# One ViT block with a mixture of experts on one core: the dense part rebuilt as one pipeline over token groups

## The chip, the cores and the metric

The kernel runs on one core of a Trainium2 chip. The metric is device time in microseconds (us), the median over runs of one execution each. TensorE is called PE below, VectorE DVE, ScalarE ACT, GpSimd POOL, and SP is the engine that issues most DMAs.

## What is computed

```python
h = patchify(x) @ W_proj.T + b_proj + pos_emb          # 16 images, 36 patches of 768 numbers, D = 256
h = concatenate([cls_tok, h])                          # 37 tokens an image, 592 in all
q, k, v = split(layernorm(h) @ Wq.T), ... Wk, ... Wv   # 4 heads of 64
attn = softmax(causal(q @ k.T)) @ v                    # within an image
sq = elu(q) + 1
A_mem = (sq @ mem) / (sq @ z + 1e-6)
out = (sigmoid(betas) * A_mem + (1 - sigmoid(betas)) * attn) @ Wo.T + bo
h = h + out
xn = layernorm(h) * gamma + beta                       # in the block: of h, then again in the experts' part
logits = xn @ router_w.T; two experts a token of 8, at most 185 tokens an expert, in token order
h = h + sum over the token's experts of weight * ((silu(xn @ Wg) * (xn @ Wu)) @ W3)
```

## The kernel before, in words

The tokens lie in 6 groups of three images: 111 rows in groups 0 to 4 and 37 in group 5. There are three stages, and each engine has its own program; they meet at semaphores alone. Everything on one engine runs in the order in which it is written.

**Embedding and value projection (lines 323 to 373 on PE).** `embed(g)` multiplies a group's patches with the patch weights: 6 slices of the 768 inputs, each as three passes (lines 335 to 337), because both sides are split into a rounded part and a rest (`x_hi` by ACT, line 611, `x_lo` by DVE, line 779). DVE adds the positions (line 800), takes mean and variance (802 to 804), POOL takes the root (986), DVE normalises into `hn` (773), PE turns it (348), ACT copies it (598) and DVE keeps the rest of it (785). `value(g)` is three passes over two slices (362 to 364). The weights of q, k and v are split too, by ACT (621) and POOL (983). The loop has group t in `embed`, t-1 in `turn_hn` and t-2 in `value`. DVE splits x two groups ahead of its sum: `x_lo` of groups 0 and 1 stands before the first `h` (793, 794).

**Query, key and memory, over all tokens (375 to 423).** Four blocks of 296 columns each for q and for k (386 to 388), the feature map on DVE and ACT, then the memory's denominator for each head as 24 small matmuls (399), its reciprocal on DVE as 111 rows of 24 numbers (850), a transpose (409), a spread over the head's 64 rows (421), and the memory's own matmul (422).

**Attention and routing (425 to 508).** A pipeline over the groups: `score` (mask and four heads), DVE's `row_max` (838), ACT's `softmax` (651), DVE's `normalise` (863 to 865), `turn_probs` (447), `attend` (457), DVE's `add_memory` (875), `project` (467), DVE's `residual` with the second statistics (882 to 888), POOL's root (1007), DVE's `norm2` (893), `turn_xn` (477), ACT's `copy_xnT` (671), `route` (484), DVE's `rank` (899 to 908), `count` (492 to 496), DVE's `send` (913 to 916), and POOL's two indirect DMAs a group (999), which put the token rows into per-expert areas in HBM. The order of each engine's stages in a step is a list of (lag, stage) pairs, written by hand:

```python
for t in range(GROUPS + 7):
    for lag, stage in ((6, route), (3, turn_probs), (4, project), (6, count), (5, turn_xn), (0, score), (3, attend)):
```

After the last group PE runs `keep_busy` (562), the rows come back (306) and the experts' stage (513 to 584) runs to the end. It starts with the transposes of line 520.

## Time and profile before

| | us |
|---|---|
| median of 3 runs | 250.87 |
| lowest, highest | 250.58, 252.39 |
| the profiled execution | 252.72 |
| its span, first to last instruction | 250.8 |
| PE busy, share of the span | 213.8, 85% |
| DVE, ACT, POOL busy | 88.2, 77.0, 55.0 |

The profile is of one execution. Its span is what the rows below are times in; 1.9 us lie outside it. Line numbers are those of the kernel before. A row of a timeline has start, duration, engine, line, operation, what it writes and reads, and in brackets the idle time before it and what ended it. Busy times of PE contain modelled ends, so a busy PE is not a PE at its peak.

### The profile page before, as it was taken

To read this page: it belongs to the slowest core of one execution; us is meant where nothing else is said; L and a number is where in the kernel's file an instruction comes from. 1 tells how busy PE (TensorE), PEld (TensorE's weight loads), DVE (VectorE), ACT (ScalarE), POOL (GpSimd) and SP (SyncE) were. 2 spreads that over 40 slices of the span, in tenths; PEclk is the share of its full clock that TensorE was granted. 3 is DMA by queue.
4 is the path that set the end of the run, shared out by engine and by line. 5 is a ranking of instruction groups with operands and counts; after the bars stand their busy time and mean duration, and the time that the engine had idled before them with its cause. 6 is when DMAs were issued, how large, how long until landed. Compare 5 with 4: busy or idle time off the path is not lost.

```text
span 250.8 us, 3563 instructions
## 1 busy us (share of the span) xinstructions
PE 213.8 (85%) x1307; PEld 189.1 (75%) x1307; DVE 88.2 (35%) x277; ACT 77.0 (31%) x226; POOL 55.0 (22%) x55
## 2 busy tenths in 40 slices
PE   0185957989998984879999999999999999999970
PEld 0175947954766553449999999999999999999960
DVE  6849874442688644302211111111211112111110
ACT  2433312632574112212722222332222323222230
POOL 0245343000004444400003104013040040220404
PEclk9999997975599555599999999999999999999997
DMA  7936995410001221157619239076191580410101
GB/s 244 332 117 130 326 347 231 210 81 1 0 21 46 90 60 49 54 148 200 259 18 400 88 136 379 4 303 231 27 432 52 199 322 0 167 11 0 22 9 16
DMA packets 10299, 36.15 MB, mean 144 GB/s; under 512 B 3328, under 2 KB 6738, under 8 KB 7978
## 3 DMA queue, kind: packets, MB, share of 16 engines
q1 hardware_dynamic: 7514, 31.90, 35.4%
q0 software_dynamic: 2336, 2.13, 4.3%
q10 hardware_dynamic: 432, 1.90, 2.0%
q8 instruction: 10, 0.16, 0.2%
q14 instruction: 7, 0.06, 0.1%
HBM read 31.42 MB, written 5.35 MB: 147 GB/s over the span
## 4 chain that ended last, share of the span: by engine, by line
PE 72%; DVE 9%; DMA 7%; issue 4%; POOL 3%; ACT 2%; POOLq 1%; SPq 1%
PE bank L536 33%; PE bank L548 16%; DMA x_flat<-in 5%; PE bank L467 3%; PE bank L520 3%; DVE hn L773 2%; PE bank L422 2%; PE bank L559 1%; POOL rstd L986 1%; POOL token_rows L999 1%; PE bank L447 1%; PE bank L386 1%; PE bank L387 1%; PE bank L388 1%; PE bank L421 1%
## 5 line engine op out<-in xcount | busy, mean ns | idle before, releaser
L536 PE MATMUL bank<-xb,w 128*128 128x185 f32 x512 | 91.4, 321 | 1.1 <-ACT xb L695 1.1
L536 PEld LDWEIGHTS bank<-xb,w 128*128 128x128 f32 x512 | 81.9, 190 | 1.6 <-issue 1.2
L957 DVE TENSOR_TENSOR hid<-bank,sg 128x185 f32<-128x185 f32 x64 | 22.5, 351 | 113.9 <-ACT sg L707 113.9
L548 PE MATMUL bank<-hid,w 128*128 128x185 f32 x256 | 50.2, 319 | 0.0
L1016 POOL DMA_INDIRECT out<-yw,slot_token x16 | 23.8, 1490 | 119.2 <-ACT yw L727 116.8
L707 ACT ACTIVATE sg<-bank 128x185 f32<-128x185 f32 x64 | 20.9, 327 | 89.1 <-PE bank L536 89.1
L548 PEld LDWEIGHTS bank<-hid,w 128*128 128x128 f32 x256 | 42.1, 189 | 0.0
L335 PE MATMUL bank<-wp_hi,x_hi 128*111 128x256 f32 x36 | 11.2, 310 | 12.6 <-DVE x_lo L779 12.6
L335 PEld LDWEIGHTS bank<-wp_hi,x_hi 128*111 128x111 f32 x36 | 7.0, 194 | 12.9 <-issue 12.9
L999 POOL DMA_INDIRECT token_rows<-rowbuf,dest x12 | 11.6, 969 | 15.1 <-DVE dest L916 13.3
L1007 POOL TENSOR_TENSOR rstd<-var,minus_half 111x1 f32<-111x1 f32 (+1 forms) x6 | 3.5, 576 | 35.0 <-DVE var L888 34.9
L336 PE MATMUL bank<-wp_lo,x_hi 128*111 128x256 f32 x36 | 10.9, 303 | 0.0
L337 PE MATMUL bank<-wp_hi,x_lo 128*111 128x256 f32 x36 | 10.9, 303 | 0.0
L467 PE MATMUL bank<-w_sb,x_flat 128*111 128x256 f32 (+1 forms) x24 | 9.9, 557 | 0.1
L695 ACT ACTIVATE xb<-bank,beta_t,gamma_t 128x185 f32<-128x185 f32 x16 | 7.2, 505 | 8.9 <-PE bank L520 8.9
L671 ACT ACTIVATE xnT<-bank,beta_t,gamma_t 128x111 f32<-128x111 f32 (+1 forms) x12 | 4.6, 433 | 15.2 <-PE bank L477 15.2
L348 PE MATMUL bank<-ident,hn 111*128 111x111 f32 (+1 forms) x12 | 2.2, 267 | 7.2 <-DVE hn L773 7.2
L986 POOL TENSOR_TENSOR rstd<-var,minus_half 111x1 f32<-111x1 f32 (+1 forms) x6 | 5.5, 913 | 11.8 <-DVE var L804 11.8
L773 DVE TENSOR_SCALAR hn<-h,mv,rstd 111x256 f32<-111x256 f32 (+1 forms) x6 | 7.5, 1243 | 1.6 <-POOL rstd L986 1.4
L651 ACT ACTIVATE x_flat<-bank,negmax 111x111 f32<-111x111 f32 (+1 forms) x24 | 7.8, 340 | 0.1
L520 PE MATMUL bank<-ident,rows_in 128*128 128x128 f32 (+1 forms) x32 | 7.5, 285 | 0.2 <-DMA rows_in<-token_rows 0.2
L520 PEld LDWEIGHTS bank<-ident,rows_in 128*128 128x128 f32 (+1 forms) x32 | 4.4, 137 | 4.1 <-issue 1.5
(139 smaller groups left out, 266.7 us busy)
## 6 DMA issues: line engine op xcount, KB each, us to landing
w<-in SPq DMA_DIRECT2D x8, 2048.0 KB, 10.2
w<-in SPq DMA_DIRECT2D x8, 1024.0 KB, 4.8
x_flat<-in SPq DMA_DIRECT2D x6, 333.0 KB, 11.0
token_rows<-rows_in SPq DMA_DIRECT2D x1, 1728.0 KB
rows_in<-token_rows SPq DMA_DIRECT2D x8, 144.0 KB
w_sb<-in ACTq DMA_DIRECT2D x1, 1024.0 KB, 8.8
wp_sb<-in ACTq DMA_DIRECT2D x1, 768.0 KB, 5.6
out<-h SPq DMA_DIRECT2D x5, 111.0 KB
```

Of the source, the lines that this page charges most:

```text
L335: pe.matmul(o, x_hi[g % 2][:, k, :], wp_hi[:, k, :], start=(k == 0), stop=False)
L336: pe.matmul(o, x_hi[g % 2][:, k, :], wp_lo[:, k, :], start=False, stop=False)
L337: mm = pe.matmul(o, x_lo[g % 2][:, k, :], wp_hi[:, k, :], start=False, stop=(k == KE - 1))
L467: mm = pe.matmul(bank[WO_BANK][0:R, 0:D], aoT[:, g % 2, k, 0:R], w_sb[:, 3, k, :], start=(k == 0), stop=(k == 1))
L520: tr = pe.transpose(bank[XB_BANK][:, k * D + s * P:k * D + s * P + n], rows_in[0:n, e, s, k * P:(k + 1) * P], ident[0:n, 0:n])
L536: mm = pe.matmul(o, w[:, part, k, :], xb[b][:, k, :], start=(k == 0), stop=(k == KD - 1))
L548: mm = pe.matmul(bank[YT_BANK[k]][:, 0:NS], w3[e % 2][:, fc, k * P:(k + 1) * P], hid[:, step % 4, :], start=(fc == 0), stop=(fc == FC - 1))
L707: act.activation(sg[:, step % 2, :], bank[GU_BANK[step % len(GU_BANK)]][:, 0:NS], ACT.Silu).then_inc(silu_done, 1)
L773: dve.tensor_scalar(hn[0:R, g, :], h[0:R, g, :], mv1[0:R, g, 0:1], rstd1[0:R, g:g + 1], ALU.subtract, ALU.mult).then_inc(hn_done, 1)
L957: dve.tensor_tensor(hid[:, step % 4, :], bank[GU_BANK[step % len(GU_BANK)]][:, NS:2 * NS], sg[:, step % 2, :], ALU.mult).then_inc(hid_done, 1)
L999: pool.indirect_dma_start(out=rows_dram, out_offset=bass.IndirectOffsetOnAxis(ap=dest[0:n, g, k:k + 1], axis=0), in_=rowbuf[0:n, g, :], in ...
L1016: pool.indirect_dma_start(out=out, out_offset=bass.IndirectOffsetOnAxis(ap=slot_token[0:n, e, s:s + 1], axis=0), in_=yw[b][s][0:n, :], in_ ...
```

## The change

The three-stage dense part becomes one loop of 9 steps. In step t a group t is embedded, group t-1 gets its query, key, value, scores and memory, group t-2 its softmax, attention and output projection, and group t-3 its routing. Every engine has one list of stages. The bank map gives most stages one bank where they had two.

- q, k, v and the memory are computed per group with plain fp32 matmuls (`w_sb`, `hnT`), so the splits of `hnT` (785) and of the q, k, v weights (621, 983) go.
- The memory's denominator is computed with a block-diagonal `z_bd`, which gives it spread over 128 rows and two head pairs. ACT copies it (`copy_den`), DVE takes the reciprocal of 128 rows of 222 numbers in `memory_part`. The gate is multiplied into `mem_bd` once (`setup`).
- The output bias, added to `h` by POOL before (991), is two one-row matmuls in `project`.
- x is split one group ahead, not two: on DVE `split_next` stands behind `first_sum`, `stats1` and `setup`.
- Six loads leave SP's queue, five are issued by ACT ahead of its first work.
- POOL's `root2(t-3)` stands behind the `send` of the step before.
- On PE `project` and `count` stand ahead of `score`; on DVE `row_max` stands last.

```diff
-        S_BANK = ((0, 1), (2, 3))
-        PT_BANK = 4
-        PV_BANK, WO_BANK = 5, 6
-        ROUTER_BANK = 7
+        PV_BANK, K_BANK, T_BANK, ROUTER_BANK, S_BANK, E_BANK, WO_BANK = 0, 1, 2, 3, (4, 5), 6, 7
+        V_BANK, Q_BANK, MEM_BANK, PT_BANK = T_BANK, E_BANK, K_BANK, WO_BANK
...
-            sp.dma_start(mask[:, :], c_mask).then_inc(in_attn, 16)
-            sp.dma_start(bo_b[:, :], bo.partition_broadcast(G_ROWS)).then_inc(in_attn, 16)
-            sp.dma_start(gate[:, :], betas.partition_broadcast(G_ROWS)).then_inc(in_attn, 16)
-            sp.dma_start(z_sb[:, :, :], z4).then_inc(in_attn, 16)
-            sp.dma_start(mem_bd[:, :, :], mem_diag).then_inc(in_attn, 16)
-            sp.dma_start(head_rows[:, :, :], c_head).then_inc(in_attn, 16)
...
             def embed(g):
+                if g >= 1:
+                    pe.wait_ge(h_copied, g)
                 if g >= 2:
-                    pe.wait_ge(h_copied, g - 1)
-                o = bank[E_BANK[g % 2]][0:G_ROWS, 0:D]
+                    pe.wait_ge(q_done, g - 1)
+                o = bank[E_BANK][0:G_ROWS, 0:D]
...
-                if g >= 2:
-                    pe.wait_ge(hnT_lo_done, g - 1)
+                if g >= 1:
+                    pe.wait_ge(v_done, g)
...
             def value(g):
-                full = slice(g * G_ROWS, (g + 1) * G_ROWS)
+                R = ROWS[g]
                 pe.wait_ge(hnT_done, g + 1)
-                pe.wait_ge(hnT_lo_done, g + 1)
                 if g == 0:
-                    pe.wait_ge(w_hi_done, 1)
-                    pe.wait_ge(w_lo_done, 1)
-                if g >= 2:
-                    pe.wait_ge(v_done, g - 1)
-                o = bank[V_BANK[g % 2]][0:G_ROWS, 0:D]
+                    pe.wait_ge(in_w, 16)
                 for k in range(KD):
-                    pe.matmul(o, hnT_hi[:, k, full], w_hi[:, 2, k, :], start=(k == 0), stop=False)
-                    pe.matmul(o, hnT_hi[:, k, full], w_lo[:, 2, k, :], start=False, stop=False)
-                    mm = pe.matmul(o, hnT_lo[:, k, full], w_hi[:, 2, k, :], start=False, stop=(k == KD - 1))
+                    mm = pe.matmul(bank[V_BANK][0:R, 0:D], hnT[:, k, cols(g)], w_sb[:, 2, k, :], start=(k == 0), stop=(k == KD - 1))
                 mm.then_inc(v_in_psum, 1)
...
+            def project_in(o, which, g):
+                R = ROWS[g]
+                for m in range(2):
                     for k in range(KD):
-                        pe.matmul(o, w_hi[:, which, k, rows], hnT_hi[:, k, half(hf)], start=(k == 0), stop=False)
-                        pe.matmul(o, w_hi[:, which, k, rows], hnT_lo[:, k, half(hf)], start=False, stop=False)
-                        mm = pe.matmul(o, w_lo[:, which, k, rows], hnT_hi[:, k, half(hf)], start=False, stop=(k == KD - 1))
-                    mm.then_inc(qk_in_psum, 1)
+                        mm = pe.matmul(o[:, m * R:(m + 1) * R], w_sb[:, which, k, m * P:(m + 1) * P], hnT[:, k, cols(g)],
+                                       start=(k == 0), stop=(k == KD - 1))
+                return mm
+            def query(g):
+                pe.wait_ge(h_copied, min(g + 2, GROUPS))
+                project_in(bank[Q_BANK], 0, g).then_inc(q_in_psum, 1)
+            def key(g):
+                if g >= 1:
+                    pe.wait_ge(mem_done, g)
+                project_in(bank[K_BANK], 1, g).then_inc(k_in_psum, 1)
+            def memory(g):
+                R = ROWS[g]
+                if g == 0:
+                    pe.wait_ge(mem_scaled, 1)
+                pe.wait_ge(k_done, g + 1)
+                pe.wait_ge(sq_done, g + 1)
+                for n, w in enumerate((mem_bd, z_bd)):
                     for m in range(2):
+                        mm = pe.matmul(bank[MEM_BANK][:, (2 * n + m) * R:(2 * n + m + 1) * R], w[:, m, :], sqT[:, m, cols(g)],
+                                       start=True, stop=True)
+                mm.then_inc(mem_in_psum, 1)
...
             def score(g):
+                if g == 0:
+                    pe.wait_ge(mask_set, 1)
+                if g >= 1:
+                    pe.wait_ge(exp_done, g)
+                pe.wait_ge(q_done, g + 1)
+                pe.wait_ge(k_done, g + 1)
...
+                    pe.wait_ge(h2_done, g)
...
             def project(g):
+                pe.wait_ge(pT_done, g + 1)
+                if g == 0:
+                    pe.wait_ge(bo_done, 2)
+                pe.matmul(bank[WO_BANK][0:R, 0:D], ones_row[:, 0:R], bo_hi[:, :], start=True, stop=False)
+                pe.matmul(bank[WO_BANK][0:R, 0:D], ones_row[:, 0:R], bo_lo[:, :], start=False, stop=False)
...
-            memory_den()
-            pe.wait_ge(k_done, 4)
-            pe.wait_ge(mask_set, 1)
-            score(0)
-            score(1)
-            memory_turn()
-            memory()
-            for t in range(GROUPS + 7):
-                for lag, stage in ((6, route), (3, turn_probs), (4, project), (6, count), (5, turn_xn), (0, score), (3, attend)):
-                    if 0 <= t - lag < GROUPS and not (stage == score and t - lag < 2):
+            for t in range(GROUPS + 3):
+                for lag, stage in ((0, embed), (3, turn_xn), (1, turn_hn), (2, turn_probs), (3, route), (1, value), (1, query), (1, key),
+                                   (2, attend), (2, project), (3, count), (1, score), (1, memory)):
+                    if 0 <= t - lag < GROUPS:
                         stage(t - lag)
...
+            act.dma_start(mask[:, :], c_mask).then_inc(in_attn, 16)
+            act.dma_start(gate[:, :], betas.partition_broadcast(P)).then_inc(in_attn, 16)
+            act.dma_start(mem_bd[:, :, :], mem_diag).then_inc(in_attn, 16)
+            act.dma_start(z_bd[:, :, :], z_diag).then_inc(in_attn, 16)
+            act.dma_start(bo_row[:, :], bo).then_inc(in_attn, 16)
...
+            act.wait_ge(in_attn, 80)
             act.activation(gate[:, :], gate[:, :], ACT.Exp, scale=-1.0).then_inc(gate_exp, 1)
...
+            def split_next(g):
+                if g + 1 < GROUPS:
+                    split_x(g + 1)
+            def copy_q(g):
+                R = ROWS[g]
+                act.wait_ge(q_in_psum, g + 1)
+                act.activation(qT[:, :, cols(g)], bank[Q_BANK][:, 0:2 * R].rearrange("p (m c) -> p m c", m=2), ACT.Copy).then_inc(q_done, 1)
+            def copy_k(g):
+                R = ROWS[g]
+                act.wait_ge(k_in_psum, g + 1)
+                act.activation(kT[:, :, cols(g)], bank[K_BANK][:, 0:2 * R].rearrange("p (m c) -> p m c", m=2), ACT.Copy).then_inc(k_done, 1)
+            def exp_q(g):
+                act.wait_ge(qneg_done, g + 1)
+                act.activation(qneg[:, :, cols(g)], qneg[:, :, cols(g)], ACT.Exp).then_inc(qexp_done, 1)
+            def copy_den(g):
+                R = ROWS[g]
+                act.wait_ge(mem_in_psum, g + 1)
+                if g >= 1:
+                    act.wait_ge(mem_done, g)
+                act.activation(den[:, :, 0:R], bank[MEM_BANK][:, 2 * R:4 * R].rearrange("p (m c) -> p m c", m=2), ACT.Identity,
+                               bias=eps_z[:, :]).then_inc(den_done, 1)
...
+            for t in range(GROUPS + 3):
+                for lag, stage in ((2, softmax), (2, copy_den), (0, split_next), (3, copy_xnT), (1, copy_hnT), (2, copy_probsT), (1, copy_v),
+                                   (1, copy_q), (1, copy_k), (1, exp_q)):
...
+            def setup(g):
+                if g != 0:
+                    return
+                dve.wait_ge(in_attn, 80)
+                dve.tensor_copy(mask_bf[:, :], mask[:, :]).then_inc(mask_set, 1)
+                dve.wait_ge(bo_done, 1)
+                dve.tensor_tensor(bo_lo[:, :], bo_row[:, :], bo_hi[:, :].bitcast(F32), ALU.subtract).then_inc(bo_done, 1)
+                dve.wait_ge(gate_exp, 1)
+                then(dve.tensor_scalar(gate[:, :], gate[:, :], 1.0, None, ALU.add))
+                then(dve.reciprocal(gate[:, :], gate[:, :]))
+                then(dve.tensor_scalar(keep[:, :], gate[0:G_ROWS, :], -1.0, 1.0, ALU.mult, ALU.add))
+                mem_heads = mem_bd[:, :, :].rearrange("p m (h c) -> p (m h) c", h=2)
+                dve.tensor_tensor(mem_heads, mem_heads, gate[:, :].unsqueeze(2).broadcast_to([P, HEADS, HD]), ALU.mult).then_inc(mem_scaled, 1)
+            def route_setup(g):
+                if g != 0:
+                    return
+                dve.wait_ge(in_ffn, 128)
+                dve.tensor_copy(rowbuf[0:G_ROWS, :, TOKEN_AT], token_info[:, :])
+                dve.tensor_copy(before_bf[:, :], before[:, :])
+                then(dve.tensor_copy(area_bf[:, :], area_row[:, :]))
+            def q_min(g):
+                dve.wait_ge(q_done, g + 1)
+                dve.tensor_scalar(qneg[:, :, cols(g)], qT[:, :, cols(g)], 0.0, None, ALU.min).then_inc(qneg_done, 1)
+            def feature(g):
+                dve.wait_ge(qexp_done, g + 1)
+                dve.scalar_tensor_tensor(out=sqT[:, :, cols(g)], in0=qT[:, :, cols(g)], scalar=0.0,
+                                         in1=qneg[:, :, cols(g)], op0=ALU.max, op1=ALU.add).then_inc(sq_done, 1)
...
+            def memory_part(g):
+                R = ROWS[g]
+                dve.wait_ge(den_done, g + 1)
+                then(dve.reciprocal(den[:, :, 0:R], den[:, :, 0:R]))
+                dve.tensor_tensor(memT[:, :, cols(g)], bank[MEM_BANK][:, 0:2 * R].rearrange("p (m c) -> p m c", m=2), den[:, :, 0:R],
+                                  ALU.mult).then_inc(mem_done, 1)
...
+            for t in range(GROUPS + 3):
+                for lag, stage in ((2, normalise), (3, norm2), (0, first_sum), (2, memory_part), (0, stats1), (0, setup), (3, rank), (0, split_next),
+                                   (1, q_min), (0, norm1), (1, feature), (2, add_memory), (1, route_setup), (3, send), (2, residual), (1, row_max)):
...
+            for t in range(GROUPS + 3):
+                for lag, stage in ((3, root2), (0, root1), (3, send)):
+                    if 0 <= t - lag < GROUPS:
...
```

## Rows read from the trace of the kernel before

**Rows 1.** Windows by stage: length; PE, PEld, DVE, ACT, POOL busy; clock; DMA share, GB/s

```profile
11.40:42.30 30.90, 22.49 (x157) 21.32 (x158) 20.80 (x46) 8.45 (x18) 14.04 (x16) 0.95 0.73 232
42.30:49.00 6.70, 6.70 (x49) 6.70 (x49) 2.96 (x11) 4.31 (x13) 0.00 (x0) 0.95 0.50 213
49.00:62.30 13.30, 12.51 (x65) 7.48 (x65) 4.33 (x16) 3.91 (x15) 0.00 (x0) 0.66 0.14 57
62.30:102.30 40.00, 32.76 (x201) 23.05 (x200) 26.08 (x115) 15.89 (x61) 13.32 (x16) 0.63 0.15 45
```

**Rows 2.** Timeline of the start: first embedding's first and last matmul, second x_lo

```profile
11.50 0.53 PE L335 MATMUL bank<-wp_hi,x_hi 128*111 128x256 f32 x1 [11.50 <-DVE x_lo L779]
...
15.24 0.41 PE L337 MATMUL bank<-wp_hi,x_lo 128*111 128x256 f32 x1
...
15.44 1.16 DVE L779 TENSOR_TENSOR x_lo<-x_flat,x_hi 128x666 fp32r<-128x666 f32 x1 [4.04 <-ACT x_hi L611]
```

**Rows 3.** Timeline of DVE: one x_lo, one run of six stages, one rank

```profile
25.26 0.84 DVE L779 TENSOR_TENSOR x_lo<-x_flat,x_hi 128x666 fp32r<-128x666 f32 x1
...
71.81 0.39 DVE L875 TENSOR_TENSOR x_flat<-bank,qneg 128x222 f32<-128x222 f32 x1
72.11 0.67 DVE L838 TENSOR_REDUCE negmax<-bank 111x2 f32<-111x222 f32 x2
...
72.90 0.41 DVE L893 TENSOR_SCALAR rowbuf<-h,mv,rstd 111x256 f32<-111x256 f32 x1
73.22 0.17 DVE L863 RECIPROCAL psums<-psums 111x4 f32<-111x4 f32 x1
...
74.16 0.42 DVE L882 TENSOR_TENSOR h<-bank,h 111x256 f32<-111x256 f32 x1
...
75.37 0.39 DVE L875 TENSOR_TENSOR x_flat<-bank,qneg 128x222 f32<-128x222 f32 x1
...
76.15 0.15 DVE L899 TENSOR_SCALAR logits<-bank 111x8 f32<-111x8 f32 x1
...
77.11 0.41 DVE L893 TENSOR_SCALAR rowbuf<-h,mv,rstd 111x256 f32<-111x256 f32 x1
```

**Rows 4.** Groups of instructions: DVE's reciprocals of 4 and of 24 columns

```profile
L863 DVE RECIPROCAL psums<-psums 111x4 f32<-111x4 f32 (+1 forms) x6 | 1.0, 167 | 0.0
...
L850 DVE RECIPROCAL den<-den 111x24 f32<-111x24 f32 x1 | 0.3, 303 | 0.0
```

**Rows 5.** Timeline of ACT: first head of a softmax, and what follows its last

```profile
73.02 0.35 ACT L651 ACTIVATE x_flat<-bank,negmax 111x111 f32<-111x111 f32 x1
...
74.35 0.79 ACT L671 ACTIVATE xnT<-bank,beta_t,gamma_t 128x111 f32<-128x111 f32 x2
```

**Rows 6.** Timeline of PE: an output projection at full clock, and the count behind it

```profile
76.06 1.03 PE L467 MATMUL bank<-w_sb,x_flat 128*111 128x256 f32 x4
77.02 0.21 PE L492 MATMUL bank<-area_bf,ones_bf 1*111 1x8 bf16 x1
```

**Rows 7.** Chain of waits: eight fp32 matmul records of 185 columns

```profile
116.28 1.26 PE bank L536 x8
```

**Rows 8.** Tail of the last group, and POOL's root: timelines, then the page's group

```profile
98.25 0.41 DVE L893 TENSOR_SCALAR rowbuf<-h,mv,rstd 37x256 f32<-37x256 f32 x1
...
102.19 0.16 DVE L916 TENSOR_REDUCE dest<-placed 37x2 uint32<-37x16 f32 x1
...
104.32 0.88 POOL L999 DMA_INDIRECT token_rows<-rowbuf,dest  x1 [0.30 <-issue]
...
L1007 POOL TENSOR_TENSOR rstd<-var,minus_half 111x1 f32<-111x1 f32 (+1 forms) x6 | 3.5, 576 | 35.0 <-DVE var L888 34.9
```

**Rows 9.** Windows before two falls of the granted clock, columns as in rows 1

```profile
34.60:39.30 4.70, 0.07 (x2) 0.01 (x1) 4.20 (x5) 0.38 (x1) 3.95 (x6) 1.00 0.91 332
77.00:80.40 3.40, 2.41 (x22) 1.71 (x21) 3.17 (x13) 1.72 (x10) 1.28 (x2) 1.00 0.04 13
```

**Rows 10.** Timeline of SP's queue: the gate's load to 111 rows

```profile
10.71 4.22 SPq L279 DMA_DIRECT2D gate<-in  x1
```

More of the change, by code:

```diff
@@ L793, in _, with split_next, first_sum @@
             split_x(0)
-            split_x(1)
-            for g in range(GROUPS):
+            def split_next(g):
+                if g + 1 < GROUPS:
+                    split_x(g + 1)
+            def first_sum(g):
                 R = ROWS[g]
@@ L1065 @@
     mem_diag = np.zeros((P, 2, P), mem.dtype)
[L1066 removed]
+    z_diag = np.zeros((P, 2, P), z.dtype)
     for n in range(HEADS):
```

264 lines of the change are left out of this document (44 added, 220 removed).

## The prediction

> **What bounds the kernel now.** I read the chain of waits first, then cut the span into windows at the stage borders of the code. The experts' stage, from its first transposes at 109.6 to the end, is PE work without gaps and is not touched; it takes as long as before, so the question is when the last group's row numbers (`dest`) are ready. Before, that is at 102.19 + 0.16 = 102.35 [rows 8]. The dense part has four stretches [rows 1]: embedding and value 30.9 us, query and key 6.7, memory 13.3, attention and routing 40.0. In none of them is an engine other than PE busy throughout, and PE's own time there is long because its clock is low: granted 0.66 and 0.63 in the last two. The reader is to see two things: 91 us pass in which DVE works 54, and PE's 74 us are at a mixed clock. So what bounds is neither engine alone but the order of dependent stages. A pipeline over everything can win what the stages lose side by side (DVE idle in the memory stretch, 4.3 of 13.3), and loses if one step's chain through DVE, ACT and PE comes out long.
>
> **The change, part by part: a step.** I walk a full step from the moment R when DVE's `row_max` of group t-2 is done to the same moment for t-1, by start-to-start distances of the rows, since DVE's stages stand in one queue and PE's too. A semaphore between engines costs about 0.05 (72.11 + 0.67, the negation, then ACT at 73.02).
>
> 1. ACT's softmax: 73.02 to 74.35 and the last sum's read, 1.45 with the semaphore [rows 5]. DVE waits, because `normalise` is first in its list and nothing stands before it.
> 2. DVE: `normalise` 73.22 to 74.16 = 0.94; `norm2` 72.90 to 73.22 = 0.32; `first_sum` 0.33, by the other 0.42 us operations less their overlap [rows 3].
> 3. `memory_part`: a reciprocal over 222 columns. The trace has 4 columns at 167 ns and 24 at 303 [rows 4], so 6.8 ns a column: 303 + 198 x 6.8 = 1.65. Bounds: 0.4, an ordinary operation of that width (0.39 in rows 3), and 2.0. I take 1.65, since two rows with one slope are nearer than another operation. The product adds 0.30. In the old kernel this reciprocal was one of 24 columns for all tokens.
> 4. `stats1` is `residual` without its sum, 1.21 - 0.42 = 0.79; `rank` 76.15 to 77.11 = 0.96; `x_lo` 0.84 less 0.08 = 0.76 [rows 3]. `rank`'s logits are there by then: turning, copy and routing take about 1.7 after `norm2` on PE and ACT.
> 5. `q_min` 0.24, then ACT's `exp_q` about 0.40 (0.35 for 111 columns in rows 5), with `norm1` beside it, then `feature` 0.30 and `add_memory` 0.39; two semaphores. Together 1.45.
> 6. PE: `project` is 76.06 to 77.02 = 0.96 [rows 6] plus two bias passes of 256 columns. Rows 2 give 18 such passes in 3.95, 0.21 each at the lower clock, so 0.11 at the higher: 1.2 with the semaphore. `count` then stands behind it, about 0.5 with the past groups' matmuls, and DVE's `send` waits for it: 0.05 + 0.37. DVE is idle for 1.75 of this. This is what the new order costs: `residual` stands behind `send`, and that behind `count`.
> 7. `residual` 74.16 to 75.37 = 1.21, `row_max` 72.11 to 72.90 and its last result, 0.88 [rows 3]. The scores are in PSUM by then: they start when `count` has, and take 0.9.
>
> The sum is 13.2; rounding overlaps down I take 13.1 for a full step. DVE works some 9.4 of it, waits 1.5 for softmax, 0.4 for `exp_q` and 1.8 for PE.
>
> Is anything else longer? PE at full clock: `embed` 18 passes, half of 3.95, 2.0; transposes 1.1; `route` 0.45; `value` 0.96; `query`, `key` and `memory` eight fp32 records each. Such a record of 185 columns takes 1.26 / 8 = 0.157 [rows 7]; 111 columns scale to 0.094 and the upper bound is 0.157, so 0.8 each, at most 1.25, and I take 0.8. With `attend` 0.5, `project`, `count` and `score` PE has about 10 of 13.1, hidden but for point 6. POOL: `send` to the end of its second scatter is 102.35 to 105.20 = 2.85, the root 0.58 [rows 8]. `root2` stands behind the `send` of the step before, so it ends about 1.6 after R, and `norm2` is reached 2.4 after R: hidden, with 0.8 to spare. Three POOL tasks that are gone (weights' rest, bias) lay beside DVE and count for nothing here.
>
> **The start.** Fewer memsets let the first `embed` start 0.35 earlier, ending at 15.24 + 0.41 - 0.35 = 15.3 [rows 2]. Before, `x_lo` of group 1 ran at 15.44, beside it. Now it stands behind `first_sum` 0.4, `stats1` 0.79 and `setup` (a cast, the bias' rest, three gate operations that wait for one another, the product with `mem_bd`: estimate 1.4). It is done at 18.75, where PE has been idle for 3.45. Step 1 then has `embed` 2.05, turn 0.3, copy 0.35, `value` 0.95, `query` 0.8, `key` 0.8, `score` and its waits 1.5, `row_max` 0.9: R(0) = 26.5. Step 2 lacks routing: 11.1, R(1) = 37.6. Then 50.7 and 63.8. Step 5 has no `x_lo` to make: 12.5, 76.3. Step 6 has a small group 5 and no embedding: 11.9, 88.2. In step 7 the way to `dest` of group 4 is 7.6: 95.8. In step 8 POOL's scatter comes first (2.85), then root 0.58, `norm2` 0.45: 99.7. From `norm2` done to the last `dest` it is 102.35 - 98.66 = 3.7 [rows 8]: 103.4. That is 1.05 later than before.
>
> **The clock.** In this kernel it fell after PE had been idle from 34.65 to 39.3, and again at 80.4, after 3.4 us of transposes, routing and gaps with PE at 2.41 of 3.40 [rows 9]. The new gap before `embed(1)` is 3.45, between that 4.65 and the 1.1 that it survived at 15.65 to 16.74. I take it that the clock falls: 18 passes at 0.21 instead of 0.11, +1.7. In every step the time after `embed` (a wait of 1.5, transposes, routing) looks like rows 9's second window, but a burst of 18 passes follows each time, and PE's long bursts in the first two rows of rows 1 kept 0.95. Some steps will have `value` to `key` at half clock, 1 us each on the path through `q_min` and `attend`; I take two such steps, +2.0. Bounds: 0 and 15 (all five steps at half, 3 each).
>
> The sum is 1.05 + 1.7 + 2.0 = +4.75. Against the profiled execution's own 252.72 (span 250.8 and 1.9 around it) that is 257.5; that execution stood 1.85 above the median, and against the median it is 250.87 + 4.75 = 255.6. I say 255.5.
>
> The Trainium skill, "VectorE: DVE Perf Modes", section on the 8-slice pipeline, says that reciprocal is an iterative divide with a repeat count of 8. As an estimate from it at the 0.96 GHz of the same skill's overview page ("Trainium Kernel Development and Optimization"), 222 columns are 1.85 us, 0.2 a step more than rows 4 give: by it the sum would be 256.6. The rows decide here.
>
> **Loads.** ACT now issues five more DMAs before its first work, some 0.4 each. Its first copy began at 6.4 after the weights had landed, and there is room of about 2. The price is nothing if none of the issues stalls; SP's queue shows that they can: the gate's load held it for 4.22 [rows 10]. If one stall of that size falls on ACT, all starts 4 later. I take 0, as that load came behind nine others and ACT's comes behind four.
>
> The Trainium skill, "DMA: Bandwidth & Descriptors", "Why a DMA increments its semaphore by 16 and not by 1", gives the engines of such a DMA as the largest number up to 16 that divides its rows: 3 for 111 rows, 16 for the new gate's 128. By it the stall is less likely on ACT; no row here shows the number of engines.
>
> **Rivals.**
> - *The clock holds* through the gap and the steps. For it: 0.95 in the first stretches. Then 251.9, no change by measure. Chance 0.22.
> - *The step is shorter (faster).* One mechanism: `memory_part`, the largest new piece on DVE's path. If the reciprocal costs 0.4, 5.3 groups save 1.25 each, 6.6: 245.3 with the clock held, 249.0 without. It decides from a reciprocal of 1.0 down, the clock held. Against it stand both rows 4. A step of 12.0 instead of 13.1 from overlaps that I don't see has the same effect, 5.5 off: 246.4. Chance together 0.27.
> - *ACT's loads stall*, 4 later: 259.6. Chance 0.13.
> - *PE stays at half clock* in the steps: `project`, `value` and `query` on the path double, 3 a step: 267. For it: 0.63 in the attention stretch before. Against it: the embedding bursts. Chance 0.08.
> - Forecast as walked, 253.5 to 258: 0.30.
>
> **How the numbers follow.** A measurement of this kernel tells about 1% from no change: faster is under 248.4, slower over 253.4. Faster 0.27, same 0.22, slower 0.51 (0.30 + 0.13 + 0.08). The range reaches from the middle of the faster cases, 246, to past the stalled loads, 264, and leaves out the half-clock case and the lowest reciprocal.
>
> **What would show it.** In the new profile: starts of DVE's `normalise` about 13 apart in steps 3 and 4; a reciprocal of 1.5 to 1.7; DVE idle for ACT before `normalise` and for PE's count before `send`; PE idle for `x_lo` before the second embedding by 3 to 4; `dest` of the last group near 107. If steps are 12 or less, or if the granted clock is 1.0 from 15 to 95, I am too high; if `wp_hi` starts after 7, the loads stalled. The forecast is wrong in kind if DVE is not the engine with the longest queue in a step.

## The result, and the profile of the changed kernel

The changed kernel takes 267.56 us (median of 4 runs, 266.44 to 269.66) against 250.73 of the kernel before on the same chip (4 runs): ratio 1.068, interval 1.061 to 1.075. The forecast was 255.5 with a range up to 264. The direction was right, the size was not.

The page's head, then the windows of the changed kernel by step, each from one start of DVE's `negmax` plus its 0.17 us (L767, the forecast's moment R) to the next, the last one to the last `dest`; columns as in [rows 1]:

```profile
span 266.3 us, 3665 instructions
...
PEclk9999999999996555559799999999999999999997
```

```profile
0.00:29.70 29.70, 13.43 (x77) 12.35 (x78) 16.27 (x36) 7.04 (x13) 4.60 (x8) 1.00 0.80 252
29.70:41.30 11.60, 9.91 (x81) 8.63 (x80) 7.71 (x22) 4.77 (x16) 1.82 (x2) 1.00 0.76 288
41.30:54.46 13.16, 10.87 (x88) 9.16 (x87) 9.11 (x31) 5.27 (x18) 1.60 (x2) 1.00 0.38 154
54.46:67.72 13.26, 10.67 (x87) 8.96 (x86) 9.16 (x31) 5.26 (x18) 3.22 (x5) 1.00 0.10 29
67.72:80.97 13.25, 10.22 (x82) 8.34 (x80) 8.39 (x30) 4.62 (x17) 3.05 (x4) 1.00 0.09 28
80.97:98.80 17.83, 14.41 (x69) 10.99 (x69) 6.75 (x24) 4.23 (x17) 2.39 (x3) 0.52 0.06 20
98.80:116.06 17.26, 8.04 (x46) 5.20 (x47) 5.93 (x29) 4.50 (x16) 4.13 (x6) 0.50 0.12 38
```

Three things are to be seen. The full steps are 13.2 long, as forecast. PE, busy for 10.2 to 10.9 (with modelled ends), is the engine with the most work in them, not DVE (8.4 to 9.2). And the granted clock, 1.0 through all steps with an embedding, is 0.5 (the lower level, 1.2 GHz) in the last two windows. The first of these is step 6, where PE's query, key and value are of the small group of 37 rows, and yet it is the longest step of all.

Now one step as each engine sees it. First DVE's timeline of step 5:

```profile
67.55 0.17 DVE L767 TENSOR_SCALAR negmax<-negmax 111x4 f32<-111x4 f32 x1
69.24 0.18 DVE L779 RECIPROCAL psums<-psums 111x4 f32<-111x4 f32 x1 [1.52 <-ACT probs L586]
...
70.19 0.41 DVE L807 TENSOR_SCALAR rowbuf<-h,mv,rstd 111x256 f32<-111x256 f32 x1
...
70.84 1.52 DVE L772 RECIPROCAL den<-den 128x222 f32<-128x222 f32 x1
...
76.22 0.38 DVE L790 TENSOR_TENSOR aoT<-bank,qneg 128x222 f32<-128x222 f32 x1
78.60 0.17 DVE L827 TENSOR_TENSOR placed<-hots,bank 111x16 f32<-111x16 f32 x1 [2.01 <-PE bank L432]
...
78.89 0.41 DVE L796 TENSOR_TENSOR h<-bank,h 111x256 f32<-111x256 f32 x1
...
80.09 0.68 DVE L764 TENSOR_REDUCE negmax<-bank 111x2 f32<-111x222 f32 x2
```

And PE's timeline of the same step, with its next wait at the end:

```profile
70.65 0.41 PE L413 MATMUL bank<-ident,rowbuf 111*128 111x111 f32 x2 [1.31 <-DVE rowbuf L807]
...
71.93 0.56 PE L420 MATMUL bank<-router_sb,xnT 128*111 128x8 f32 x4 [0.29 <-ACT xnT L606]
72.34 1.10 PE L323 MATMUL bank<-w_sb,hnT 128*111 128x256 f32 x4
73.27 1.93 PE L330 MATMUL bank<-hnT,w_sb 128*128 128x111 f32 x16
75.14 0.60 PE L390 MATMUL bank<-probsT,v_sb 111*64 111x111 f32 x8
76.65 0.36 PE L400 MATMUL bank<-bo_hi,ones_row 1*111 1x256 f32 x1 [0.91 <-DVE aoT L790]
...
78.37 0.19 PE L432 MATMUL bank<-hot,before_bf 111*111 111x8 bf16 x1
...
78.73 0.64 PE L370 MATMUL bank<-kT,qT 64*111 64x111 f32 x8
...
83.90 0.63 PE L413 MATMUL bank<-ident,rowbuf 111*128 111x111 f32 x2 [3.44 <-DVE rowbuf L807]
```

Read together they are a ring. PE starts its work after the embedding with `turn_xn`, which needs `norm2` (70.19 to 70.65). `norm2` stands in DVE's queue behind `normalise`, which waits for ACT's softmax, which waits for the row maximum; that stands behind `residual` and so behind `count`, and the scores themselves behind `project` and `count` on PE. From `turn_xn` to the end of `attend` PE works with one gap of 0.29 (70.65 to 75.74). In step 6 there is no embedding, PE's wait for `norm2` grows from 1.31 to 3.44, and that is where the clock falls (granted 0.92 from 80 to 82, 0.50 from 82 to 84).

The tail, in DVE's timeline and POOL's: the root of group 5 stands behind the two scatters of group 4.

```profile
112.31 0.40 DVE L807 TENSOR_SCALAR rowbuf<-h,mv,rstd 37x256 f32<-37x256 f32 x1 [2.51 <-POOL rstd L895]
...
115.90 0.16 DVE L830 TENSOR_REDUCE dest<-placed 37x2 uint32<-37x16 f32 x1
```

```profile
109.44 0.98 POOL L903 DMA_INDIRECT token_rows<-rowbuf,dest  x1 [8.69 <-DVE dest L830]
110.73 0.94 POOL L903 DMA_INDIRECT token_rows<-rowbuf,dest  x1 [0.30 <-issue]
111.70 0.57 POOL L895 TENSOR_TENSOR rstd<-var,minus_half 37x1 f32<-37x1 f32 x1
```

The start, on DVE and PE (the first embedding's last pass, then three of the second embedding's first four):

```profile
15.84 0.42 DVE L720 TENSOR_TENSOR h<-bank,pos 111x256 f32<-111x256 f32 x1 [4.66 <-POOL pos L885]
...
18.45 0.85 DVE L704 TENSOR_TENSOR x_lo<-x_flat,x_hi 128x666 fp32r<-128x666 f32 x1
```

```profile
15.01 0.41 PE L303 MATMUL bank<-wp_hi,x_lo 128*111 128x256 f32 x1
19.44 0.53 PE L301 MATMUL bank<-wp_hi,x_hi 128*111 128x256 f32 x1 [4.01 <-DVE x_lo L704]
...
19.98 0.42 PE L303 MATMUL bank<-wp_hi,x_lo 128*111 128x256 f32 x1
20.19 0.42 PE L301 MATMUL bank<-wp_hi,x_hi 128*111 128x256 f32 x1
```

The passes start 0.21 apart where full clock gives 0.12 (the last embedding: 68.83, 68.94, 69.06), though the window's granted clock reads 1.00. A pass of 256 columns in 0.213 is 1.2 GHz, so here the pace is the better witness. The first embedding's passes are 0.21 apart as well (14.59, 14.80, 15.01). The Trainium skill, "TensorE: Matmul & The Clock Gate", "Seeing it yourself", says that the clock events of a trace have been seen to be unreliable; these rows agree.

### The profile page after: what moved, and what is told of

Same layout as the page of the kernel before. It is cut to its first block, busy times and chain, and to the rows that moved or that the text cites. A ratio compares the mean times of both kernels' runs of the same rounds, so it can differ in the third digit from the quotient of the medians.

```text
span 266.3 us, 3665 instructions
## 1 busy us (share of the span) xinstructions
PE 217.4 (82%) x1361; PEld 195.4 (73%) x1361; DVE 88.1 (33%) x275; ACT 76.0 (29%) x230; POOL 46.6 (17%) x46
## 4 chain that ended last, share of the span: by engine, by line
PE 67%; DVE 12%; DMA 7%; ACT 5%; issue 4%; POOL 3%; POOLq 1%; SPq 1%; ACTq 0%; DVEq 0%
PE bank L465 31%; PE bank L477 15%; DMA bias<-in 5%; PE bank L330 4%; PE bank L403 3%; ACT probs L586 3%; PE bank L449 2%; PE bank L323 2%; PE bank L488 1%; PE bank L420 1%; DVE probs L781 1%; DVE negmax L764 1%; ACT xnT L606 1%; PE bank L413 1%; POOL token_rows L903 1%
## 5 line engine op out<-in xcount | busy, mean ns | idle before, releaser
L465 PE MATMUL bank<-xb,w 128*128 128x185 f32 x512 | 93.1, 326 | 1.1 <-ACT xb L621 1.1
L465 PEld LDWEIGHTS bank<-xb,w 128*128 128x128 f32 x512 | 83.5, 193 | 1.6 <-issue 1.2
L301 PE MATMUL bank<-wp_hi,x_hi 128*111 128x256 f32 x36 | 12.2, 340 | 15.3 <-DVE x_lo L704 15.3
L586 ACT ACTIVATE probs<-bank,negmax 111x111 f32<-111x111 f32 (+1 forms) x24 | 7.9, 341 | 28.5 <-DVE negmax L767 28.5
L413 PE MATMUL bank<-ident,rowbuf 111*128 111x111 f32 (+1 forms) x12 | 2.9, 334 | 13.8 <-DVE rowbuf L807 13.8
L330 PEld LDWEIGHTS bank<-hnT,w_sb 128*128 128x128 f32 x96 | 13.3, 215 | 1.1 <-issue 0.8
L330 PE MATMUL bank<-hnT,w_sb 128*128 128x111 f32 (+1 forms) x96 | 13.4, 297 | 0.0
L413 PEld LDWEIGHTS bank<-ident,rowbuf 111*128 111x128 f32 (+1 forms) x12 | 1.5, 172 | 14.9 <-DVE rowbuf L807 14.9
L890 POOL TENSOR_TENSOR rstd<-var,minus_half 111x1 f32<-111x1 f32 (+1 forms) x6 | 4.7, 791 | 32.0 <-DVE var L727 32.0
L403 PE MATMUL bank<-w_sb,aoT 128*111 128x256 f32 (+1 forms) x24 | 8.4, 485 | 0.0
```

Source lines behind the costliest of these rows:

```text
L301: pe.matmul(o, x_hi[g % 2][:, k, :], wp_hi[:, k, :], start=(k == 0), stop=False)
L330: mm = pe.matmul(o[:, m * R:(m + 1) * R], w_sb[:, which, k, m * P:(m + 1) * P], hnT[:, k, cols(g)], start=(k == 0), stop=(k == KD - 1))
L403: mm = pe.matmul(bank[WO_BANK][0:R, 0:D], aoT[:, g % 2, k, 0:R], w_sb[:, 3, k, :], start=False, stop=(k == 1))
L465: mm = pe.matmul(o, w[:, part, k, :], xb[b][:, k, :], start=(k == 0), stop=(k == KD - 1))
L586: a = act.activation(probs[0:R, t % 2, hd, 0:R], bank[S_BANK[hd % 2]][0:R, (hd // 2) * R:(hd // 2 + 1) * R], ACT.Exp, bias=negmax[0:R, t, ...
```

## The experiments

The theory after the comparison: two losses, the half clock from step 6 on and the ring through softmax and routing. The rivals: DVE's queue (as forecast), POOL's place for the root, the start. All ratios are to runs of the kernel before on the same chip, 4 runs of the variant unless said; differences in us between variants are of medians, some of them across chips.

**The clock at the end.** Filler passes of PE (expert weights multiplied with themselves into an unused part of a bank; PE waits for those weights ahead of step 5) ahead of `turn_xn` in steps 6, 7 and 8, and eight passes ahead of the experts.

```diff
+            def warm(t):
+                for n in range({6: 7, 7: 5, 8: 9}.get(t, 0)):
+                    pe.matmul(bank[E_BANK][:, 256:512], w12[0][:, 0:P], w12[0][:, 0:256], start=True, stop=True)
...
+                    if stage == turn_xn:
+                        warm(t)
...
-            keep_busy(5)
+            keep_busy(8)
```

> PE gets extra matmuls whose results nobody reads, in the waits of steps 6, 7 and 8 (7, 5 and 9 of 256 columns, ahead of the routing's transposes), and 8 instead of 5 such passes before the experts' stage. Theory (the granted clock falls at the end of the loop and stays low; that is the part of the loss that my walk left out): the clock stays 1.0 from 80 to the experts' stage, the distance from the last row maximum of group 4 to that of group 5 falls from 17.9 us to about 12, the last dest from 116.1 to about 108, the experts' first matmuls run at full pace (1.7 less), in all 8 to 10 us faster than the changed kernel, about 258. Rival (the last steps are long because each waits for DVE and POOL, and PE's pace is not on the path): within 1 us of 267.6.

262.68, ratio 1.048 (1.036 to 1.060): 4.9 less than the changed kernel. The clock held at 1.0 until 99, and step 6 took 12.76 instead of 17.83 (`negmax` of groups 4 and 5 at 82.15 and 94.91). In steps 7 and 8 the gain is small: step 7 to `dest` took 9.26 instead of 9.84, and step 8 took 8.01 instead of 7.42, because the clock had fallen again and the nine passes there, 5.59 us at the lower clock, held PE until 109.38, when the rows that it turns next had been ready since 108.42. The stretch from the last `dest` to the end is 2.2 shorter. And the clock also fell in step 2 of this run, at 38, where the changed kernel kept it. PE's timeline of this run, then of the changed kernel:

```profile
37.96 0.37 PE L400 MATMUL bank<-bo_hi,ones_row 1*111 1x256 f32 x1 [1.46 <-DVE aoT L798]
```

```profile
37.65 0.37 PE L400 MATMUL bank<-bo_hi,ones_row 1*111 1x256 f32 x1 [1.46 <-DVE aoT L790]
```

The instructions up to there are the same and so is the idle time. The clock's history is not: in this run the first embedding's passes had already gone from 0.21 to 0.12 apart at 14.65 and were at 0.21 again at 19.54; in the changed kernel both embeddings ran at 0.21 throughout. The windows behind it, of this run and of the changed kernel:

```profile
38.00:40.00 2.00, 2.00 (x6) 1.43 (x7) 0.00 (x0) 0.00 (x0) 0.00 (x0) 0.62 0.46 197
```

```profile
38.00:40.00 2.00, 2.00 (x17) 1.48 (x16) 0.75 (x2) 0.00 (x0) 0.00 (x0) 1.00 0.53 225
```

So after a gap of the same length the clock fell in one execution and not in the other. The Trainium skill, "TensorE: Matmul & The Clock Gate", "What's actually happening", says of the warming at a kernel's start that it is "run-variable"; these rows show the same of a fall in the middle. So the theory stands for step 6 (5.1 of the expected 6) and for the experts' stage; it doesn't for step 8, and 1.05 of the gain was lost in step 2, which took 12.65 instead of 11.60.

**The start.** The second group's split ahead of the loads' exponential on ACT and of the first sum on DVE.

```diff
             split_x(0)
+            split_x(1)
...
-                if g + 1 < GROUPS:
-                    split_x(g + 1)
+                if g + 2 < GROUPS:
+                    split_x(g + 2)
```

> x is split two groups ahead again, on ACT and on DVE, all else as changed. Theory (the second embedding waited for its x_lo behind the first group's sum, statistics and setup, and PE fell to half clock in that gap): the second embedding starts at about 16.6 instead of 19.4 and its 18 passes take 2.1 instead of 3.9, so 4 to 4.6 us faster, about 263.3. Without the clock's part it would be 2.8. Rival (the start is hidden behind later waits): under 1 us.

266.38 over 5 runs, ratio 1.063 (1.053 to 1.072): a miss. `x_lo` came at 17.03 instead of 18.45 and the second sum at 21.51 instead of 23.63, but the first `negmax` at 29.69 against 29.53. The 2.1 us were given back at once, with PE at the lower clock through value, query and key: 2.05 and 2.77 us instead of 1.12 and 1.93. The second embedding's passes had started 0.12 apart and were at 0.21 again from 19.6 on. PE began them at 18.27, when the first sum, now behind `x_lo` on DVE, had left the bank free. Here the earlier start alone gained nothing.

**DVE's reciprocal.** This kernel multiplies the denominator by one instead of inverting it, so its memory part is another value.

```diff
-                then(dve.reciprocal(den[:, :, 0:R], den[:, :, 0:R]))
+                then(dve.tensor_scalar(den[:, :, 0:R], den[:, :, 0:R], 1.0, None, ALU.mult))
```

> The reciprocal of the memory's denominator is left out: DVE multiplies the same 128 rows of 222 by one instead, so the memory's part is multiplied by its denominator. Theory (DVE's queue is the step's path up to q_min): the operation takes about 0.3 instead of 1.5, each full step is about 1.2 shorter until the exp of q binds, some 0.8 of it counts, 4 to 6 us in all, about 262.5. Rival (q_min waits for PE's query anyway): 0 to 1.5 us in all, since in steps 3 and 4 q_min follows the query's copy by only a little.

266.14, ratio 1.064 (1.054 to 1.075). The groups of instructions, the changed kernel first, then this one:

```profile
L772 DVE RECIPROCAL den<-den 128x222 f32<-128x222 f32 x5 | 7.6, 1529 | 0.0
```

```profile
L772 DVE TENSOR_SCALAR den<-den 128x222 f32<-128x222 f32 x5 | 1.3, 265 | 0.0
```

1.26 us less work for DVE in every full step, and the full steps stay at 13.1 to 13.3 (`negmax` at 53.80 and 67.07); only step 2, which has no routing, falls, from 11.60 to 10.98. ACT's timelines show why. `exp_q`, which `add_memory` needs through `feature`, stands behind `copy_k`, and that waits 0.54 for PE's key. From the start of `norm2` to `copy_k` it is 5.06 in both kernels (56.99 to 62.05, and here 56.50 to 61.56). DVE's queue is not the path between `norm2` and `add_memory`; the forecast's central claim falls here, and the rival of the expectation (0 to 1.5 us) holds.

**The scores ahead of the projection,** with `row_max` right behind `add_memory`.

```diff
-                                   (2, attend), (2, project), (3, count), (1, score), (1, memory)):
+                                   (2, attend), (1, score), (2, project), (3, count), (1, memory)):
...
-(2, add_memory), (1, route_setup), (3, send), (2, residual), (1, row_max)):
+(2, add_memory), (1, row_max), (1, route_setup), (3, send), (2, residual)):
```

> The order inside a step is turned: on PE score stands ahead of the output projection and the count, on DVE row_max stands ahead of send and residual. Theory (the order is what makes a step long: DVE is idle 2 us for projection and count, and then softmax starts only after residual and row_max): the row maximum moves into that wait, softmax runs beside residual, the step falls from 13.2 to about 10.8 us, 10 to 12 us faster in all, about 256.5. Rival (the step is bound by the sum of DVE's work): about 9.5 of DVE's work and no gain beyond 1 us per step, 262 or more.

263.33, ratio 1.051 (1.037 to 1.064). The step without routing falls from 11.6 to 8.75 (`negmax` 29.04, 37.79) and the next from 13.16 to 10.7, but the following are 12.95 and 12.4. Softmax is hidden, and now something else is late. DVE's timeline and POOL's:

```profile
66.62 0.41 DVE L807 TENSOR_SCALAR rowbuf<-h,mv,rstd 111x256 f32<-111x256 f32 x1 [1.55 <-POOL rstd L895]
```

```profile
63.75 0.99 POOL L903 DMA_INDIRECT token_rows<-rowbuf,dest  x1 [5.57 <-DVE dest L830]
65.04 0.94 POOL L903 DMA_INDIRECT token_rows<-rowbuf,dest  x1 [0.30 <-issue]
66.01 0.58 POOL L895 TENSOR_TENSOR rstd<-var,minus_half 111x1 f32<-111x1 f32 x1
```

The root waits behind two scatters of the group before, as in the tail of the changed kernel.

**The same with the root ahead of the send.**

```diff
-                for lag, stage in ((3, root2), (0, root1), (3, send)):
+                for lag, stage in ((0, root1), (2, root2), (3, send)):
```

> The run with the scores ahead of the projection, and one more change: POOL's list has the routing root ahead of the send's two scatters, as (root1, root2, send). Theory (once routing runs, the step is the chain routing root, normalised rows, their turning at the head of PE's list, and the root was late only because it stood behind the send): DVE's wait for the routing root goes, full steps take about 11 us instead of 12.4 to 12.9, the last step's wait of 2.5 goes too, the time is about 257. Rival (POOL's place is not what sets these steps): full steps stay at 12.4 to 12.9 and the time at 263.

253.82, ratio 1.016 (1.012 to 1.021): better than expected, 13.7 under the changed kernel (5.2% by the ratios). The windows of two full steps:

```profile
48.63:59.74 11.11, 10.50 (x85) 8.92 (x86) 9.11 (x31) 5.47 (x18) 3.37 (x4) 1.00 0.21 70
59.74:70.77 11.03, 10.73 (x87) 9.17 (x88) 8.39 (x29) 4.72 (x17) 3.05 (x4) 1.00 0.11 35
```

PE is busy for 10.5 of 11.11 and 10.7 of 11.03: the step is now close to PE's own work.

**The root ahead of the send alone.** The edit of the last diff on the changed kernel.

> The changed kernel with POOL's order alone edited: (root1, root2, send). Theory (two late edges of one ring, scores behind the projection and the root behind the send; the slower of the two sets the step): the full step stays at 13.2 because PE's order still sets it, and only the tail, where DVE waited 2.5 us for the root, gets shorter: about 264.5. Rival (the root's place alone was the fault): full steps of about 11 us and about 257.

264.26, ratio 1.051 (1.044 to 1.059). Full steps are still 13.2 (`negmax` 54.00, 67.20, 80.45), and the wait of 2.5 in the tail is gone (last `dest` 113.25 instead of 115.90). So the two orders don't add: alone they give 4.2 and 3.3 (1.7% and 1.6% by the ratios), together 13.7. In each lone edit the other edge holds the full step.

**All lists in another order.** PE takes the group in attention first, then turns, then routing; the other engines follow, and the root stands ahead of the send. Only PE's list is shown.

```diff
+                for lag, stage in ((0, embed), (1, turn_hn), (1, value), (1, query), (1, key), (2, turn_probs), (3, turn_xn), (3, route),
+                                   (1, score), (2, attend), (2, project), (3, count), (1, memory)):
```

> All lists of a step put in another order: PE takes the group in attention first (turning, value, query, key) and the routing group's products behind them, scores ahead of attend and project; ACT, DVE and POOL follow. Theory (the full step of 13.2 us is PE's chain through rows that routing needs, not the sum of any engine's work): no routing product stands between the embedding and the value product, full steps take about 10.5 to 11 us, the time is about 255 without any filler. Rival (the step is DVE's queue, as the prediction had it): DVE's busy time of a step is the same, full steps stay at 12.5 or more, the time at 262 or above.

268.81, ratio 1.076 (1.071 to 1.081): a miss. The steps are 13.3 again (65.10 to 78.47), since PE now waits 0.45, 0.29, 1.11 and 0.72 for copies that stand further back on ACT and DVE, and DVE 2.48 for the routing. The time is the one that the rival (DVE's queue) gave, but DVE waits for 4.4 of this step. Bringing one group's work forward on PE moved other copies back. Four lists changed at once, so no single move is shown to be the fault. With fillers as well (2, 4 and 5 late ones, 16 in the start) it is worse:

> The reordered lists together with filler passes of TensorE: 16 between the first two embeddings, 2, 4 and 5 in steps 6 to 8, and 8 instead of 5 ahead of the experts. Theory (order of a step and clock in the last steps are two losses that add): about 5 us below the run with the reordered lists alone, at about 250. Rival (with shorter steps PE never idles long enough to lose its clock, so the fillers only cost): no gain, or up to 2 us slower than the reordered lists alone.

276.32, ratio 1.108 (1.100 to 1.117). Here and in the next run the fillers bring a wait that was not meant: the one for the first expert weight stands ahead of step 3 instead of 5, and PE waits 4.79 there (3.18 in the next run) for that transfer. Both say little about the end; their starts can be read.

**Fillers in the start too,** 16 passes between the first two embeddings.

```diff
+                if t == 1:
+                    for n in range(16):
+                        pe.matmul(bank[7][:, 0:D], wp_hi[:, 0, 0:P], wp_hi[:, 0, :], start=True, stop=True)
```

> The run with filler passes in steps 6 to 8, and one more change: 16 filler passes of TensorE between the first and the second embedding (they leave the result as it is). Theory (the second embedding runs at half pace because PE stood idle ahead of it): its products take about 0.12 us each instead of 0.21, the first step is about 2 us shorter, the time goes from 262.7 to about 261. Rival (what comes late in the start is the data, not the clock): the first scores come within 0.5 of before and the time stays at 262.7.

265.64, ratio 1.062 (1.053 to 1.071). The theory's first half is right: the second sum comes at 21.83 instead of 23.63 and the first `negmax` at 27.63 instead of 29.53, with the passes 0.12 apart. The time got worse than with late fillers alone: step 3 takes 19.6, with that wait of 3.18 and the embedding behind it at 0.21 a pass again. The clock had fallen at about 38, but step 2 itself kept its 11.6. One thing more can be read: here the clock stayed at 1.00 in step 7 until 105, and the step took 7.9 to `dest`, instead of 9.84 in the changed kernel and 7.6 in the forecast.

**Both orders with fillers.** Late ones alone (4, 6 and 6 passes, 8 ahead of the experts):

> Scores ahead of the projection and routing root ahead of the send, as in the run before, with filler passes of TensorE in steps 6, 7 and 8 (4, 6 and 6) and 8 instead of 5 ahead of the experts; they leave the result as it is. In the run without them the granted clock is 0.50 from 76 to 108 us of the span. Theory (that half clock costs part of what is left): the first row maximum of group 5 comes at about 82 instead of 84.7, the last dest at about 99 instead of 103.2, the time is about 250. Rival (at these shorter steps the tail hangs on DVE, ACT and the scatters and a faster PE only waits): within 1 us of 253.8.

251.72 over 10 runs, ratio 1.000 (0.995 to 1.005). In its profile the first `negmax` came 1.3 later than in the run without fillers: 0.7 because the first sum, which waits for POOL's positions, came at 16.20 instead of 15.46, and 0.5 because `value` ran at the lower clock (1.5 instead of 0.95; both second embeddings ran at 0.21 a pass). And yet group 5's `negmax` came at 82.17 instead of 84.73. Against the run without fillers, step 6 is 3.8 shorter (10.12 instead of 13.95) and step 7 is 1.45 shorter, but step 8 is 1.8 longer and the stretch from the last `dest` 1.3 longer. With the 1.3 of the start that makes the 0.9 between the two spans (251.5 and 250.6); in the medians it is 2.1, and by the ratios, since the two ran on different chips, 1.6%. Then with 16 passes in the start, their wait now before step 5:

> The run with both orders and the late fillers, and also 16 filler passes between the first two embeddings. Theory: the second embedding runs at full pace and everything behind it comes about 1.9 us sooner, as the first row maximum did in the run that had both kinds of filler; there the gain was lost again, since PE also had to wait for an expert weight at step 3, which is not so here: about 248. Rival (the gain is lost to a fall of the clock in step 2, as in two runs with fillers): no gain over the run with late fillers alone.

249.72 over 10 runs, ratio 0.996 (0.990 to 1.001); first `negmax` 27.76. Last, with 12 passes in the start and the second group split ahead:

> The same with 12 filler passes in the start, and the second group split ahead of the loads' exponential on ACT and ahead of the first sum on DVE. Theory (the start loses to both the order of the splits and the clock, and the run with the splits ahead alone gave its 2.1 us back because the clock stayed low): the second sum comes at about 20 instead of 21.8, the time about 1.5 us under the run with 16 fillers. Rival (the attention's loads set the first scores): the first row maximum no earlier than 27.6 and no gain.

248.58, ratio 0.988 (0.981 to 0.996). The second sum came at 21.23, not 20, and the first `negmax` at 27.42 is a third of a microsecond sooner. This is the fastest version, the only one here whose interval lies under the kernel before. Its page's clock row, for comparison with the one above:

```profile
PEclk9999999999999957899999999999999999999997
```

The late fillers still lose in step 8. PE's and DVE's timelines of this run:

```profile
89.94 5.02 PE L436 MATMUL bank<-w 128*128 128x256 f32 x12
94.89 0.31 PE L413 MATMUL bank<-ident,rowbuf 37*128 37x37 f32 x2
```

```profile
92.34 0.41 DVE L820 TENSOR_SCALAR rowbuf<-h,mv,rstd 37x256 f32<-37x256 f32 x1 [0.69 <-POOL rstd L908]
```

The rows of group 5 are ready at 92.75, but the six passes ahead of their transpose, mostly at the lower clock, last until 94.96. Step 8 takes 7.44 where the run without fillers takes 5.60. No run leaves out these six passes alone.

## Why the prediction was wrong

Walk and trace, both without any charge for the clock:

| | forecast | measured | difference |
|---|---|---|---|
| R(0) | 26.5 | 29.70 | +3.2 |
| step 2 | 11.1 | 11.60 | +0.5 |
| steps 3, 4 | 13.1, 13.1 | 13.16, 13.26 | +0.2 |
| step 5 | 12.5 | 13.25 | +0.75 |
| step 6 | 11.9 | 17.83 | +5.9 |
| step 7, to `dest` of group 4 | 7.6 | 9.84 | +2.2 |
| step 8, to the last `dest` | 7.6 | 7.42 | -0.2 |
| last `dest` to the end of the span | 148.45 | 150.24 | +1.8 |

The differences sum to 14.4; with the walk's +1.05 that is the 15.5 between the spans (266.3 and 250.8). Of it the forecast had charged 4.75.

**The step that failed is the clock.** The forecast put +2.0 on two full steps and nothing behind step 5. It was the other way round: the clock held in every full step, where a burst of 18 passes follows each gap, and fell in step 6, the first without an embedding. Steps 6 and 7 give 8.1 of the 14.4; with the clock held, step 6 took 12.76 (late fillers) and step 7 took 7.9 (fillers at both ends), so 7.0 of the 8.1 is the clock. The forecast had written the reason down itself ("a burst of 18 passes follows each time") and not asked in which steps the burst is missing. What remains of step 6, 0.9, stays unexplained. In whole runs the late fillers gave 4.9 and, with the orders mended and 4, 6 and 6 passes, 2.1 (253.82 to 251.72); both carry what the fillers cost in step 8.

The number 267 of the rival "PE stays at half clock in the steps" fits the measured 267.56 by luck: its mechanism, full steps at half clock, did not occur.

**The start was undersized by 1.5.** The second embedding at half pace was forecast at +1.7 and confirmed: passes 0.21 apart, and 1.9 sooner with fillers in the gap. Its reason was not quite right: there was no fall in the gap of the profiled execution, as the first embedding's passes were at 0.21 already. The forecast read [rows 2] as the lower clock in point 6 and then took the clock as held through the old gap of 1.1; in the trace of before the passes are 0.21 apart ahead of that gap and 0.12 behind it, so it rose there. The rest of the +3.2 is data: `first_sum` at 15.84 waits for POOL's sum, DVE reaches `x_lo` at 18.45 and PE begins at 19.44 against the forecast 18.75, and `value` to `row_max` took longer than walked. ACT's loads did not stall: `wp_hi` starts at 6.95 against 6.4 before, so that rival falls, though the exponential of the gate, behind the first `x_hi` on ACT, waited 7.15 for the last of these loads.

**The full step's length was right, its reason wrong,** so the hit is luck in part. The sum of 13.1 met 13.2, and so did its terms on DVE: a reciprocal of 1.53 against 1.65, waits of 1.52 for softmax and 2.01 for `count` against 1.5 and 1.8. By the repeat count in the Trainium skill ("VectorE: DVE Perf Modes", section on the 8-slice pipeline) the estimate was 1.85; the trace decides for the slope of [rows 4]. But between `norm2` and `add_memory` two chains of almost equal length run side by side, DVE's own and PE's through `turn_xn`, routing, value, query and key to `copy_k` and `exp_q` on ACT. The forecast added up the first and set PE's ten microseconds aside as hidden. Two findings contradict it: the reciprocal's 1.26 gave nothing, and step 5, forecast 0.6 shorter for want of an `x_lo`, was not shorter. The rival "the reciprocal is cheaper, 6.6 faster" would thus have been wrong even with its price met. In the forecast's own words it is wrong in kind, since PE has the longest work in a step.

**What the new order costs** was named in point 6, and is the larger part: the wait for softmax, and `residual` behind `count`. What the forecast didn't see is that both belong to one ring, that scores ahead of the projection open it, and that the root's 0.8 to spare is then gone (with the scores first, DVE waits 1.55 for it). The run with both orders is 13.7 us better than the changed kernel; of the 14.8 between their spans (266.3 and 251.5) 0.4 comes from the start, 9.7 from steps 2 to 5 (51.3 in the changed kernel, 41.6 there), 2.6 from the tail and 2.1 from the experts' stage.

**POOL in step 8** was as walked: two scatters, root, `norm2` done 4.1 after `dest` of group 4, against 3.9.

**The experts' stage** took 1.8 longer with nothing changed in it. In the changed kernel PE had ended its filler passes and waited 1.40 for the rows, and the granted clock was 0.76 at 124 to 128. With eight passes instead of five (the first experiment) the stretch from the last `dest` is 148.05, with five and both orders, where PE had no wait there and the clock stayed at 1.0 from the rows' arrival on, it is 148.1. The lone root order kept the clock too, at 148.4. So the 1.8 goes with the clock, by comparison and not by an edit of its own. Eight passes are not better as such: in the last three runs they began at the lower clock, took 8.83, and the experts' first product started 10.2 after the last `dest` instead of 8.9, so that the stretch is 149.4 there.

What stays open: no run shows why a gap of 1.46 keeps the clock once and loses it once, nor what the last version would take without its passes in step 8 and with five ahead of the experts.

## What to carry to other kernels

In a pipeline written as lists per engine, look for the ring: a stage at the head of one engine's list that needs a result from the tail of another's. Its length and not any engine's busy time is the step, and where two edges close it, mending one shows little (4.2 and 3.3 here) and both show much (13.7). Sum every engine's chain between two meeting points before one is called the path. And ask of the clock step by step what fills PE's gaps: the steps at a pipeline's end lack the stage that kept it busy, and some otherwise useless passes there are worth their time where they end before the next real product could start (step 6 here); where they run past that, at the lower clock, they cost more than they give (step 8 here).

## What the runs showed of the hardware

- The granted clock in the windows reads 1.00 from 11 to 24 us while passes of 256 columns start 0.213 apart, the pace of 1.2 GHz; with fillers in the gap before them they start 0.12 apart. The Trainium skill, "TensorE: Matmul & The Clock Gate", "Wait — 56ns, not 53.3ns?", gives columns over 1.2 GHz for the one and columns over 2.4 GHz and 2.5 ns for the other: 0.213, which the trace meets, and 0.109, where it shows 0.118.
- After the same idle time of 1.46 us, behind the same instructions but with another clock at the start, the clock fell in one execution and not in another; the run that lost it took 12.65 instead of 11.60 for that step.
- fp32 products of small width don't get cheaper: a query or key record of the 37-column group took 0.22 us at the lower clock (16 in 3.56), one of 111 columns 0.12 at the higher (16 in 1.93). A third of the columns at half the pace would be 0.08. At the higher clock, in the run with late fillers, the 16 records of 37 columns took 1.91 us, as long as those of 111.
- DVE's reciprocal took 1.529 us for 222 columns and 0.607 for 74: 6.2 ns for each column more, and some 0.15 beside.
